# A fused attention and gated feed-forward kernel on one core: five hand-written order tables are replaced by five others

## The reference, cut to what matters

```python
x  = L0_attn_x                              # 4 x 512 x 256, float32
xn = layernorm(x)
q, k, v = (xn @ Wq.T, xn @ Wk.T, xn @ Wv.T)      # 16 heads of 16
att = q @ k.T / sqrt(16) + causal mask           # for each head, 512 x 512
s = softmax(att) @ v  -> 4 x 512 x 256 -> @ Wo.T
W = (wq.astype(float32) - 128) * scale[:, None]  # for gate, up (704 x 256) and down (256 x 704)
f = (silu(xn @ Wgate.T) * (xn @ Wup.T)) @ Wdown.T
out = x + s * silu(f)
```

## Time and profile before

| what | value |
|---|---|
| time, median of 3 runs (lowest to highest) | 272.1 us (271.79 to 272.63) |
| the profiled execution | 272.11 us |
| its span in the trace | 270.4 us |
| TensorE (PE) busy | 262.4 us, 97% of the span |
| TensorE weight loads (PEld) | 199.8 us, 74% |
| VectorE (DVE) | 205.8 us, 76% |
| ScalarE (ACT) | 175.8 us, 65% |
| GpSimd (POOL) | 135.6 us, 50% |

### The profile page before, as it was taken

How to read it: one execution, slowest core, us unless ns; L and a number is a source line. 1 busy time by engine, 2 the same in 40 slices (tenths; PEclk the granted TensorE clock), 3 DMA queues, 4 the chain that set the end, 5 groups by cost and what they waited for, 6 DMA issues and landing times.

```text
span 270.4 us, 5822 instructions
## 1 busy us (share of the span) xinstructions
PE 262.4 (97%) x2060; PEld 199.8 (74%) x2060; DVE 205.8 (76%) x715; ACT 175.8 (65%) x260; POOL 135.6 (50%) x235
## 2 busy tenths in 40 slices
...
GB/s 255 333 244 215 161 78 6 1 105 191 91 57 108 15 0 6 121 190 85 54 76 2 120 1 5 39 121 102 136 7 92 148 0 2 4 6 80 80 0 78
DMA packets 18004, 23.09 MB, mean 85 GB/s; under 512 B 2936, under 2 KB 11064, under 8 KB 17976
## 3 DMA queue, kind: packets, MB, share of 16 engines
...
...
## 4 chain that ended last, share of the span: by engine, by line
PE 85%; DVE 4%; SPq 3%; POOL 2%; DMA 2%; ACT 1%; issue 1%; POOLq 0%
PE ps L427 16%; PE ps L429 14%; PE ps L428 14%; PE ps L588 14%; PE ps L553 10%; PE ps L571 9%; PE ps L598 3%; DMA xin<-in_x 2%; PE ps L607 1%; PE ps L560 1%; SPq L365 1%; PE ps L470 1%; DVE wdl L982 1%; PE ps L540 1%; PE ps L541 1%
## 5 line engine op out<-in xcount | busy, mean ns | idle before, releaser
L1022 DVE CUSTOM_DVE_ANT_0 ps<-ps,maskt 128x512 f32<-128x512 f32 (+3 forms) x256 | 117.6, 523 | 15.5 <-PE ps L553 15.4
L868 POOL TENSOR_SCALAR_AFFINE_SELECT pt<-pt 128x256 f32<-128x256 f32 (+1 forms) x112 | 47.3, 439 | 81.3 <-ACT pt L795 80.1
L795 ACT ACTIVATE pt<-ps 128x1024 f32<-128x1024 f32 x80 | 78.9, 1026 | 10.8 <-PE ps L571 10.1
L844 POOL TENSOR_TENSOR hid<-hid 128x512 f32<-128x512 f32 x24 | 31.8, 1327 | 17.4 <-ACT hid L744 12.4
L588 PE MATMUL ps<-pt,vt 128*32 128x256 f32 (+3 forms) x528 | 37.8, 427 | 0.0
L1022 DVE DVE_READ_ACCUMULATOR2_ANT mx<- 128x1 f32 x256 | 36.2, 141 | 0.0
L553 PE MATMUL ps<-kp,qp 64*128 64x512 f32 (+3 forms) x256 | 33.3, 343 | 0.9 <-DVE mx L1022 0.8
L571 PE MATMUL ps<-qp,kp 64*128 64x512 f32 (+3 forms) x256 | 31.2, 335 | 0.0
L588 PEld LDWEIGHTS ps<-pt,vt 128*32 128x32 f32 x528 | 15.5, 109 | 21.1 <-issue 15.6
L848 POOL TENSOR_TENSOR hl<-hid,hh 128x512 fp32r<-128x512 f32 x20 | 26.9, 1346 | 3.9 <-ACT hh L752 3.5
L427 PE MATMUL ps<-xh,guh 128*128 128x512 f32 x66 | 28.4, 431 | 0.1
(11 more groups left out here) (128 smaller groups left out, 511.8 us busy)
## 6 DMA issues: line engine op xcount, KB each, us to landing
...
```

Source lines behind the costliest of these rows:

```text
L795: nc.scalar.activation(pair(b, s), ps[:, b0:b1 + 1:b1 - b0, :], ACT.Exp, scale=SCALE).then_inc(exp_done, 1)
L844: nc.gpsimd.tensor_tensor(a, a, hid[:, m % 2, 1, :], ALU.mult).then_inc(h_done, 1)
L868: mm = nc.gpsimd.affine_select(out=diag, in_=diag, compare_op=ALU.is_ge, fill=0.0, base=0, pattern=[[0, diag.shape[1]], [1, P]], channel_m ...
L1022: mm = nc.vector.tensor_tensor_reduce(part, part, maskt[:, T - wide:], -1.0, TOP, ALU.add, ALU.min, mg[:, e, a // 2, i:i + 1])
```

## The change

Only the five tables are replaced; no function is touched. The same units stand in each table, in another order, and the PSUM banks of nearly all units of TENSOR_ORDER are others. The line of TENSOR_ORDER in which the third maxima unit of batch 0 stands, and the places of `wds`, `wdh`, `wlo`, `wdl` and `wol` in the two other tables:

```diff
 TENSOR_ORDER
-gu:0:5:2 gu:0:6:0 gu:0:7:3 gu:0:8:2 m:0:2:17 m:0:3:03 gu:0:9:4 gu:0:10:1 t:1:0:5 m:0:4:06 m:0:5:37 v:0:0:4 m:0:6:02
+qk:0:3:7 gu:0:6:3 gu:0:7:2 gu:0:8:4 m:0:2:35 m:0:3:01 m:0:4:26 gu:0:9:7 gu:0:10:3 v:0:0:0 t:1:0:1 t:1:1:2 m:0:5:47
 SCALAR_ORDER
-tanh:0:0 up:0:0 pkal:0:0 tanh:0:1 qhi:0:3 xn:1:0 up:0:1 hhi:0:0 wdh:0:0 hhi:0:1 xn:1:1 tanh:0:2 up:0:2 tanh:0:3
+qhi:0:2 pkal:0:0 up:0:0 tanh:0:1 wdh:0:0 up:0:1 xn:1:0 hhi:0:0 xn:1:1 hhi:0:1 xn:1:2 tanh:0:2 xn:1:3 tanh:0:3 up:0:2
 VECTOR_ORDER
-bn:1:2 bn:1:3 mom:1:0 wds:0:0 qlo:0:0 gate:0:0 qlo:0:1 qlo:0:2 gate:0:1 qlo:0:3 wol:0:0 maxa:0:0 maxb:0:0 wdl:0:0
-gate:0:2 maxa:0:1 gate:0:3 maxb:0:1 wlo:0:2 maxa:0:2 maxb:0:2 maxa:0:3 maxb:0:3 gate:0:4 maxa:0:4 gate:0:5 maxb:0:4
+bn:1:2 bn:1:3 mom:1:0 qlo:0:0 wds:0:0 qlo:0:1 gate:0:0 gate:0:1 wlo:0:2 wdl:0:0 qlo:0:2 wol:0:0 maxa:0:0 maxb:0:0
```

More of the change, by code:

```diff
@@ L74 @@
[L74 to L88, removed]
@@ new lines @@
+hhi:2:0 qhi:2:2 tanh:2:1 exp:1:10 zcp:1:1 exp:1:11 exp:1:12 ccp:1:3 up:2:1 exp:1:13 tanh:2:2 hhi:2:1 exp:1:14 up:2:2
+zhi:1:0 tanh:2:3 hhi:2:2 ccp:2:0 qhi:2:3 exp:1:15 zcp:1:2 exp:1:16 exp:1:17 exp:1:18 exp:1:19 up:2:3 tanh:2:4
+exp:2:0 hhi:2:3 zcp:1:3 exp:2:1 exp:2:2 vcp:2:0 vcp:2:1 exp:2:3 zhi:1:1 ccp:2:1 up:2:4 exp:2:4 hhi:2:4 exp:2:5
+zcp:2:0 exp:2:6 exp:2:7 ccp:2:2 exp:2:8 exp:2:9 tanh:2:5 xhi:3:0 xhi:3:1 exp:2:10 up:2:5 zcp:2:1 exp:2:11 exp:2:12
+hhi:2:5 exp:2:13 qhi:3:0 tanh:3:0 zhi:2:0 ccp:2:3 fth:2:0 qhi:3:1 qhi:3:2 fth:2:1 exp:2:14 exp:2:15 up:3:0 hhi:3:0
@@ L90 @@
+zcp:2:2 exp:2:16 qhi:3:3 tanh:3:1 up:3:1 tanh:3:2 exp:2:17 exp:2:18 hhi:3:1 ccp:3:0 up:3:2 exp:2:19 hhi:3:2 tanh:3:3
+exp:3:0 vcp:3:0 zcp:2:3 up:3:3 exp:3:1 exp:3:2 ccp:3:1 tanh:3:4 exp:3:3 exp:3:4 vcp:3:1 zhi:2:1 exp:3:5 hhi:3:3
+zcp:3:0 exp:3:6 exp:3:7 up:3:4 exp:3:8 ccp:3:2 exp:3:9 tanh:3:5 up:3:5 hhi:3:4 exp:3:10 hhi:3:5 zcp:3:1 exp:3:11
+exp:3:12 exp:3:13 exp:3:14 ccp:3:3 fth:3:0 zhi:3:0 zcp:3:2 exp:3:15 exp:3:16 exp:3:17 exp:3:18 exp:3:19 fth:3:1
+zcp:3:3 zcp:3:4 zhi:3:1 zhi:3:2
 """
@@ L97 @@
[L97 to L106, removed]
@@ L112 @@
-maxb:3:10 maxa:3:11 maxb:3:11 maxa:3:12 maxb:3:12 maxa:3:13 maxb:3:13 gate:3:4 maxa:3:14 maxb:3:14 maxa:3:15
-maxb:3:15 sh:3:2 norm:3:0 gate:3:5 maxa:3:16 maxb:3:16 maxa:3:17 maxb:3:17 hlt:3:0 fin:2:0 maxa:3:18 maxb:3:18
-fin:2:1 maxa:3:19 maxb:3:19 sh:3:3 norm:3:1 u:3:0 zlo:3:0 norm:3:2 u:3:1 norm:3:3 norm:3:4 zlo:3:1 zlo:3:2 fin:3:0
-res:3:0 fin:3:1 res:3:1
+bn:1:2 bn:1:3 mom:1:0 qlo:0:0 wds:0:0 qlo:0:1 gate:0:0 gate:0:1 wlo:0:2 wdl:0:0 qlo:0:2 wol:0:0 maxa:0:0 maxb:0:0
+maxa:0:1 gate:0:2 gate:0:3 maxb:0:1 qlo:0:3 maxa:0:2 maxb:0:2 maxa:0:3 maxb:0:3 gate:0:4 maxa:0:4 gate:0:5 maxb:0:4
@@ new lines @@
+maxb:1:3 maxa:1:4 maxb:1:4 maxa:1:5 maxb:1:5 sh:1:0 norm:0:2 gate:1:3 maxa:1:6 maxb:1:6 maxa:1:7 maxb:1:7 maxa:1:8
+maxb:1:8 gate:1:4 maxa:1:9 maxb:1:9 maxa:1:10 maxb:1:10 sh:1:1 norm:0:3 zlo:0:1 gate:1:5 fin:0:0 xlo:2:0 fin:0:1
+xlo:2:1 maxa:1:11 maxb:1:11 maxa:1:12 maxb:1:12 hlt:1:0 maxa:1:13 maxb:1:13 gate:2:0 qlo:2:0 qlo:2:1 maxa:1:14
+maxb:1:14 sh:1:2 maxa:1:15 maxb:1:15 maxa:1:16 maxb:1:16 u:1:0 norm:1:0 u:1:1 maxa:1:17 maxb:1:17 maxa:1:18
+maxb:1:18 qlo:2:2 maxa:1:19 maxb:1:19 gate:2:1 maxa:2:0 maxb:2:0 maxa:2:1 sh:1:3 maxb:2:1 maxa:2:2 maxb:2:2 maxa:2:3
@@ new lines @@
+maxb:2:3 norm:1:1 maxa:2:4 maxb:2:4 gate:2:2 sh:2:0 zlo:1:0 gate:2:3 maxa:2:5 maxb:2:5 maxa:2:6 qlo:2:3 maxb:2:6
+norm:1:2 maxa:2:7 maxb:2:7 maxa:2:8 maxb:2:8 gate:2:4 maxa:2:9 maxb:2:9 sh:2:1 norm:1:3 maxa:2:10 maxb:2:10
+maxa:2:11 maxb:2:11 zlo:1:1 maxa:2:12 maxb:2:12 maxa:2:13 fin:1:0 maxb:2:13 maxa:2:14 maxb:2:14 sh:2:2 fin:1:1
+norm:2:0 maxa:2:15 maxb:2:15 gate:2:5 xlo:3:0 xlo:3:1 maxa:2:16 maxb:2:16 maxa:2:17 maxb:2:17 norm:2:1 hlt:2:0
+maxa:2:18 maxb:2:18 maxa:2:19 maxb:2:19 sh:2:3 qlo:3:0 gate:3:0 zlo:2:0 u:2:0 qlo:3:1 qlo:3:2 maxa:3:0 maxb:3:0
@@ new lines @@
+u:2:1 maxa:3:1 maxb:3:1 maxa:3:2 maxb:3:2 maxa:3:3 maxb:3:3 maxa:3:4 maxb:3:4 qlo:3:3 sh:3:0 gate:3:1 maxa:3:5
+maxb:3:5 gate:3:2 norm:2:2 maxa:3:6 maxb:3:6 maxa:3:7 maxb:3:7 maxa:3:8 maxb:3:8 gate:3:3 maxa:3:9 maxb:3:9 sh:3:1
+norm:2:3 maxa:3:10 maxb:3:10 maxa:3:11 maxb:3:11 gate:3:4 maxa:3:12 maxb:3:12 maxa:3:13 maxb:3:13 zlo:2:1 maxa:3:14
+maxb:3:14 sh:3:2 norm:3:0 maxa:3:15 maxb:3:15 gate:3:5 maxa:3:16 maxb:3:16 maxa:3:17 maxb:3:17 hlt:3:0 maxa:3:18
+maxb:3:18 fin:2:0 fin:2:1 maxa:3:19 maxb:3:19 sh:3:3 norm:3:1 u:3:0 zlo:3:0 norm:3:2 u:3:1 norm:3:3 norm:3:4 zlo:3:1
@@ L116 @@
+zlo:3:2 fin:3:0 res:3:0 fin:3:1 res:3:1
 """
 GPSIMD_ORDER = """
-init3:0:0 rows:0:3 vones:0:0 rows:0:4 rows:0:5 sc:0:0 root:1:0 root:1:1 root:1:2 root:1:3 hid:0:0 hid:0:1 hlo:0:0
-hlo:0:1 hid:0:2 hid:0:3 hlo:0:2 hlo:0:3 hid:0:4 hid:0:5 hlo:0:4 root:2:0 root:2:1 mask:0:0 mask:0:1 root:2:2
-root:2:3 mask:0:2 mask:0:3 mask:0:4 mask:0:5 mask:0:6 mask:0:7 hid:1:0 mask:0:8 hlo:1:0 mask:0:9 mask:0:10 mask:0:11
-mask:0:12 hid:1:1 mask:0:13 root:3:0 mask:0:14 root:3:1 root:3:2 hlo:1:1 hid:1:2 mask:0:15 root:3:3 hlo:1:2
```

101 lines of the change are left out of this document (54 added, 47 removed).

## The result

The changed kernel took 275.1 us (median of 4 runs, 274.39 to 276.02), the one before 272.0 beside it (271.99, 4 runs): ratio 1.0112, 95% interval 1.0073 to 1.0152. That lies outside the range of 270.6 to 273.6 and on its slow side.

The account below looks back on a forecast made before the run. The prediction took TensorE's summed work to bound the middle and GpSimd's chain to end the head. Head -0.3, changes of form +1.0 and waits -0.5 gave +0.2 on 272.1, so 272.3 us, range 270.6 to 273.6.

Parts of the forecast that it names:

- The price of a change of form: TensorE, middle: switching between matmul forms costs 0.20 us each; five more changes there cost +1.0 us.
- The 0.5 that better waits should give back: Middle: of 1.5 us of waits at TensorE's weight loads, a third counted as gained, -0.5 us.
- the four instructions named: Head: VectorE lines 974, 956, 982 with 983, and 967 run beside GpSimd's root and hold its steps.
- the forecast 3.7: Head: losses of GpSimd's root under VectorE's holds, 3.7 us, so it ends at 25.9, 1.7 later.
- one wait of 2 us in place of today's 0.7 and 0.8: Head, TensorE before the third maxima unit: waits from near 30.4 for gate:0:3 at 32.5.
- GpSimd's chain: Head: root, then hid and hl pieces to 41.8, VectorE line 1006 to 42.5, when da:0:0 starts.
- the forecast's bracket: Head: TensorE's 9.7 us to da:0:0: eight units of 0.34, twelve matmuls of 0.23, 24 of 0.12, two transpositions of 0.45.
- the forecast 42.5: End of the head: da:0:0 starts at 42.5 instead of 42.76, -0.3 us.
- The one with the root held for the full length of the holds: Slower rival, head: root ends at 27.0, da:0:0 at 43.6, 273.4 us; chance 0.17.
- The two in which the time falls: Faster rivals: head freed, 270.6 us, chance 0.17; waits of the middle go, 271.1 us, chance 0.11.
- that of net new waits in the middle: Slower rival: middle gets 0.1 us or more of net new waits, +0.9 and up, about 273.2 us; chance 0.10.
- The second of the faster ones: Rival, middle: searched order spreads maxima better, waits go: -0.3 + 0.8 - 1.5 = -1.0, 271.1 us; chance 0.11.

Follow-up runs that it names:

- e6: Head orders of before joined to the changed kernel's rest, head banks renumbered so that they meet free ones: 272.59 us, ratio 1.0008.
- e12: Before with 36 added matmuls of form 128*128 between pairs of maxima units: 288.60 us; 275.55 us with the same matmuls in form 64*128.
- e4: Changed kernel with GpSimd's memsets of the spare rows ahead of the four scale instructions again, as in before: 274.61 us, ratio 1.0077.
- e5: Changed kernel with 13 matmuls on zeros filling TensorE's wait ahead of the third maxima unit: 273.62 us, ratio 1.0046.
- e13: Changed kernel with VectorE's wlo:0:2 ahead of the statistics, wol behind the first shift, wdl directly ahead of gate:0:2: 273.84 us, ratio 1.0053.
- e9: Changed kernel with VectorE's wlo:0:2 ahead of the statistics, wol behind the first shift, wdl behind maxb:0:3: 273.12 us, ratio 1.0037.
- e2: Changed kernel's orders up to the first down projection, then those of before: 279.31 us, ratio 1.0249.

## Why the prediction was wrong, step by step

**What bounds the kernel, and the middle.** Right: the middle is TensorE's sum and came out at +0.37 us by the traces and +0.3 by e6, whose interval also holds zero, where +0.5 was forecast. The price of a change of form was right (0.20 forecast, 0.18 measured). The 0.5 that better waits should give back is not shown: the loads' waits for named engines are 22 and 7.1 us now, 20 and 6.1 before; of the ten rows of after the first and the last:

```profile
PEld ps L571 <- DVE mx L1022: 1.8, 5, 0.4
...
PEld ps L598 <- ACT zbuf L773: 0.2, 1, 0.2
```

Five changes at 0.18 are 0.9, so something gave 0.5 back, or these five cost less than the ones of e12, which all stand between maxima units; which it was stays open.

**The root.** Right in kind: the four instructions named hold it, and it ends late. The size was off: 25.9 forecast, 26.75 measured. In the change's own trace the steps slipped through between the holds, as forecast, and the holds cost 3.2 us, 0.5 less than the forecast 3.7. What made it later than forecast there is its start, 1.33 later than the 17.77 that the forecast took over, though the order of the change has the memsets moved. But an early start would not have given the forecast either: in e4 the root starts at 17.78, the holds cost 4.2 (one step took 2.36 us across three VectorE instructions, where the forecast let a step through in each), and it ends at 26.48, 0.58 over the forecast. So both terms were wrong, and how long the holds last differs from trace to trace.

**The step that failed.** It was this one: "one wait of 2 us in place of today's 0.7 and 0.8. From there its work to da:0:0 takes some 9.7 ... and ends at 42.2, within the chain." The wait was 3.02. Behind it the work took 11.0 us instead of 9.7 (33.29 to 44.28), since the clock fell, and it was not within GpSimd's chain but set the end: the last maxima came late, line 1006 behind them. At full clock the length of that work does hold: in e5 it takes 9.8 from 33.51 on, though da:0:0 waits 0.42 more for the same line there. (The terms in the forecast's bracket add up to 9.3, not 9.7, and count eight short units of 0.34 where seven of some 0.41 stand; that the total fits is luck.) No term stood for the clock, because no row of before's head or middle shows it low; yet the tail's 0.94 showed that it can fall, and a wait more than twice as long as either in the head was priced as its length alone.

The Trainium skill (TensorE: Matmul & The Clock Gate, Part 1) says that the throttled level is the default and that activity releases it, so that a pause can cost more than its length. The traces agree where the clock fell: 0.54 behind 3.02 us, 0.61 behind 1.81 us, full when the same pause is filled (e5). But it was full, too, behind pauses of 2.07 us (e13), 1.85 (e9) and 2.85 (e2), so the length of a pause alone does not tell.

**The sum for this head.** Root 0.85 late, of which 0.79 reach the gate (33.29 for 32.5); clock 1.16; line 1006 behind the queue 0.25 (44.70 less 42.5, 0.79 and 1.16). Together 2.2 over the forecast 42.5. The median is 0.7 above the profiled execution, by the clock of the other runs.

**The rivals.** The one with the root held for the full length of the holds came nearest (root 27.0, 273.4): its condition, a root that ends after 26.5, was met, and its price was 1.7 short, about the clock's share. The condition came about by the late start, not by holds in full. The two in which the time falls, and that of net new waits in the middle, did not happen. (The second of the faster ones takes the changes of form at 0.8 where the sum has 1.0, and the one of new waits adds up to +0.8, not +0.9; neither bears on the outcome.)
